# Token stages with two norms: ScalarE's second root placed ahead of the copies of the older chunk's projections

## The chip, the cores and the metric

The kernel runs on one core of a Trainium2 chip. The metric is the device time of one execution in microseconds, as the median of several executions of the same program. An engine is named as the profile names it: PE is TensorE (PEld its weight loads), ACT is ScalarE, DVE is VectorE, POOL is GpSimd, SP is SyncE.

## The reference, cut to what matters

Two decoder layers work on x of shape (2, 1024, 256), 2048 tokens in all. Each layer adds to the residual, in turn, a self-attention, a cross-attention on a context of 77 tokens, and a feed-forward part. The last part of the second layer normalises twice: the layer norm in front of it, and an RMS norm inside it.

```python
def _layernorm(x, axis=-1, eps=1e-05):
    m = jnp.mean(x, axis=axis, keepdims=True)
    v = jnp.var(x, axis=axis, keepdims=True)
    return (x - m) / jnp.sqrt(v + eps)

def _rmsnorm(x, w):
    xf = x.astype(jnp.float32)
    rms = jax.lax.rsqrt(jnp.mean(xf * xf, axis=-1, keepdims=True) + EPS)
    return (xf * rms).astype(x.dtype) * w

x = x + _L1_xattn_ref(_layernorm(x), ctx_1024, ctx_1024, mask, ...)
x = x + _L1_ffn_ref(_layernorm(x), ...)
# inside _L1_ffn_ref, with h the layer-normed x that it was given:
# q, k, v = rmsnorm(h, ln1_w) @ wq.T, wk.T, wv.T, 16 heads of 16
```

What the change touches is this place: the residual after the cross-attention's output projection is layer-normed, kept as `Y`, RMS-normed, and projected to queries, keys and values.

## The kernel before, in words

The program is a chain of stages with a barrier after each. Token stages (`token_stage`, tags t0 to t6) carry out everything that is done token by token between two attentions: the output projection of the attention behind, the residual sum, the norm or norms, the projections for the attention ahead. Between them lie attention stages (a0, a1, a3, a4, a5) and expert stages (e2, e6).

A token stage goes through eight chunks of 256 tokens (two tiles of 128). Each engine runs its own program of steps, written by `in_stages` (L83): a step is given three chunks, the newest, the one before it and the one before that. The order of the work on an engine is the order of the lines in that engine's `step`; between engines only semaphores order it. In step n:

- **PE** (block from L626): output projection of chunk n into `psY` (L649); then the feature units of chunk n-2 (L672) and its value rows (L677) into banks `psP`; then the transposes of chunk n-1 (L691). In DVE's and ACT's counting, where the newest chunk is the one that is being normalised, PE makes `psY` one chunk ahead of it.
- **DVE**: residual sum (L836), moments of the newest chunk (L810, L813), in stages with parts the remainder `rr` of the oldest chunk (`rest`, L905), reciprocal of the root (L824), the first normalisation (L855), and with two norms the moments of its result (L810 and L813 again, and for an RMS norm mean squared plus variance, L816 and L818), the second reciprocal (L824), the second normalisation (L880); then the copies of the middle chunk's values out of `psP` (L942). Each step ends in a drain.
- **ACT**: `root(front, 0)` (L703), `second_part` of the oldest chunk (L756), `keep` (L709: the kept copy `Y`), `projections` of the middle chunk, `root(front, 1)` (L703 again), `turned_rows` (L768 and L770, in other stages L765).
- **POOL**: `store_sets` of the oldest chunk: it waits for ACT's `second_part`, subtracts for the third part (L484) and issues the stores (L488); then the store of the middle chunk's values (L502).
- **SP**: loads of the attention's rows, and late in the stage the first loads of the next one.

`projections(middle)` reads each feature unit's bank twice per unit: once to `fo` (L740, f32) and once to `parts` (L742, bf16), and the second gives the bank back (`act_free`). Before the copies it waits for `rest_ready` and for the older stores from the same buffer.

Queries, keys and values of a chunk make six jobs on PE (four feature units, two halves of the values), on RP = 4 banks. So a job waits until the job four before it has been emptied:

```python
if not (c == 0 and n < RP):
    pe.wait_ge(*freed(back, n - RP))
```

`freed` counts ACT's semaphore for feature units and DVE's for values. `root` waits for the moments and writes `sd`, which DVE's `inverse_root` waits for:

```python
act.wait_ge(var_ready, c * passes + q + 1)
act.activation(sd[:], src, ACT.Sqrt, bias=G["eps"][:]).then_inc(sd_ready, 1)
```

`passes` is 2 for two stages. t2 (`norm="ln_ln"`) has a gate and no feature units: `units` is empty and NS is 0. t5 (`norm="ln_rms"`) has four feature units (queries and keys, two each), values of 256 columns, and a kept `Y`. t5 runs from about 1918 to 2005 us of the profiled span.

Of the kernel before, what the change touches and what calls it, by code (L numbers as in the profile page):

```python
# [379 lines left out]
def token_stage(nc, G, tag, weights, *, norm, attn=None, resid=None, units=(), wide=None, heads_group=4, hd=16, outs=None,  # L380
# [14 lines left out]
    passes = 1 if norm in ("ln", "rms") else 2  # L395
    dve_frees = [u >= n_units + n_rot for u in range(NU)]

    with Stage(nc, tag) as st:
# [122 lines left out]
        with st.block() as block:  # L521
# [175 lines left out]
            def _(act):  # L697
                def root(front, q):

                    c, p, r = front  # L700
                    act.wait_ge(var_ready, c * passes + q + 1)
                    src = mv[:, :, 1:2] if not (norm == "rms" or (norm == "ln_rms" and q)) else ms[:, :, 1:2]
                    act.activation(sd[:], src, ACT.Sqrt, bias=G["eps"][:]).then_inc(sd_ready, 1)  # L703

                def keep(front):

                    c, p, r = front
                    act.wait_ge(xn_ready if norm == "ln_ln" else kept_ready, c + 1)
                    act.activation(G["Y"][:, bass.ds(c * CT, CT), :], xn[p][:], ACT.Copy).then_inc(y_kept, 1)  # L709
# [35 lines left out]
                def first_part(back):  # L745

                    c, p, r = back
                    act.wait_ge(rotated, c + 1)
                    wait(act, f_out[p], r * store_per_use)
                    act.activation(parts[p][:, :, 0, :], fo[p][:], ACT.Copy).then_inc(first_cast, 1)  # L750

                def second_part(back):

                    c, p, r = back
                    act.wait_ge(rest_ready, c + 1)
                    act.activation(parts[p][:, :, 1, :], rr[p][:], ACT.Copy).then_inc(second_cast, 1)  # L756

                def turned_rows(front):

                    c, p, r = front  # L760
                    act.wait_ge(turned, c + 1)

                    wait(act, pu_ready, (c - 1) * NU)
                    if fsc is None:
                        act.activation(xT[p][:].rearrange("p k (t q) -> p t k q", q=P), psX[p][:], ACT.Copy  # L765
                                       ).then_inc(xT_ready, 1)
                    else:
                        act.activation(xT[p][:, 0, :].rearrange("p (t q) -> p t q", q=P), psX[p][:, :, 0, :],  # L768
                                       ACT.Copy, scale=fsc[:, 0:1])
                        act.activation(xT[p][:, 1, :].rearrange("p (t q) -> p t q", q=P), psX[p][:, :, 1, :],  # L770
                                       ACT.Copy, scale=fsc[:, 1:2]).then_inc(xT_ready, 1)

                def step(front, middle, back):
                    in_parts = NS and wide is None
                    if front:
                        root(front, 0)
                    if back and in_parts and not rope:
                        second_part(back)
                    if front and keep_y:
                        keep(front)  # L780
                    if middle:
                        projections(middle)
                    if front and passes == 2:
                        root(front, 1)
                    if back and rope:
                        first_part(back)
                    if front:
                        turned_rows(front)
                    if back and rope:
                        second_part(back)  # L790

                in_stages(step)
                if NS and wide is None:
                    store_last(act, 1)
# [2054 lines left out]
```

## Time and profile before

| what | value |
|---|---|
| median of 3 runs | 2729.84 us |
| lowest and highest of them | 2726.03 and 2733.44 us |
| the profiled execution's own time | 2742.19 us |
| its span in the profile | 2740.5 us |
| PE busy | 2372.9 us, 87% |
| DVE busy | 1609.1 us, 59% |
| ACT busy | 1132.7 us, 41% |
| POOL busy | 1024.0 us, 37% |

The span runs from the first to the last instruction; the execution's own time has a little around it (1.7 us). Busy shares are means over stages that have different limits, so for a change inside one stage its timeline is what counts. In a timeline a row gives the start, the length of the stretch, engine, line, operation, what is written and read, how many instructions were merged into the row, and in brackets the idle time before it with what ended it.

### The profile page before, as it was taken

How to read it: one execution, taken by the hardware profiler on the slowest of the kernel's cores; microseconds unless marked ns; L12 is line 12 of the kernel's file. 1: busy time of each engine (PE TensorE's matmuls, PEld its weight loads, DVE VectorE, ACT ScalarE, POOL GpSimd, SP SyncE). 2: the span in 40 equal slices, each digit the busy share in tenths (PEclk: the TensorE clock that was granted, in tenths of full speed). 3: DMA queues.
4: the chain of work that ended last, by engine and by line, in shares of the span. 5: the costliest groups of instructions: out<-in, count | busy, mean ns of one | idle time of the engine just before them, and what ended most of it. 6: DMA issues, size and time to landing. Idle time of an engine off the chain costs nothing. (4 is left out here: it accounts for less than half of the span.)

```text
span 2740.5 us, 44861 instructions
## 1 busy us (share of the span) xinstructions
PE 2372.9 (87%) x16088; PEld 1261.4 (46%) x16088; DVE 1609.1 (59%) x2652; ACT 1132.7 (41%) x2058; POOL 1024.0 (37%) x799
## 2 busy tenths in 40 slices
PE   6688997777897986999999999867869999968998
PEld 5533335245786762333333333732622222247887
DVE  6778864664443324666666664356779999663222
ACT  3446664331002331444444444233536777812221
POOL 3621004212441113776777777131440000015665
PEclk9889998567999997999999999965979999969999
DMA  4432203438995562122222221433431211046665
GB/s 148 133 83 63 73 20 95 95 93 242 332 334 157 192 204 91 59 91 79 70 86 82 84 73 52 152 109 71 123 107 38 58 39 37 13 117 184 187 194 147
DMA packets 233134, 315.50 MB, mean 115 GB/s; under 512 B 56838, under 2 KB 173856, under 8 KB 232447
## 3 DMA queue, kind: packets, MB, share of 16 engines
q1 hardware_dynamic: 192412, 243.02, 28.1%
q0 software_dynamic: 35232, 66.39, 10.1%
q10 hardware_dynamic: 5314, 3.78, 0.6%
q8 instruction: 107, 1.75, 0.3%
q14 instruction: 69, 0.56, 0.1%
HBM read 215.59 MB, written 96.83 MB: 114 GB/s over the span
## 5 line engine op out<-in xcount | busy, mean ns | idle before, releaser
L1731 ACT ACTIVATE a_probs<-a_cols 128x512 f32<-128x512 f32 (+3 forms) x896 | 445.2, 549 | 242.4 <-PE a_cols L1669 161.8
L1745 DVE TENSOR_REDUCE a_mxw<-a_rows 128x2 f32<-128x1024 f32 (+1 forms) x448 | 475.1, 1098 | 63.4 <-PE a_rows L1627 38.4
L2179 DVE TENSOR_REDUCE a_mxw<-a_rows 128x2 f32<-128x1024 f32 x256 | 313.3, 1224 | 207.9 <-PE a_rows L2007 206.1
L2158 ACT ACTIVATE a_probs<-a_cols 128x1024 f32<-128x1024 f32 x256 | 261.5, 1024 | 267.0 <-PE a_cols L2036 249.5
L1988 POOL TENSOR_TENSOR a_sums<-a_sums,a_probs 128x1024 f32<-128x1024 f32 x128 | 309.7, 2420 | 103.5 <-ACT a_probs L2158 90.9
L2483 PE MATMUL e_psU<-e_xT,e_w 128*128 128x128 f32 (+1 forms) x1472 | 253.0, 331 | 11.6 <-issue 8.3
L2483 PEld LDWEIGHTS e_psU<-e_xT,e_w 128*128 128x128 f32 x1472 | 229.0, 195 | 33.6 <-issue 13.8
L1988 POOL TENSOR_TENSOR a_sums<-a_probs 128x1024 f32<-128x1024 f32 x64 | 150.2, 2347 | 92.7 <-ACT a_probs L2158 92.7
L1669 PE MATMUL a_cols<-a_qs,a_ks 50*128 50x512 bf16 (+7 forms) x1120 | 172.1, 360 | 4.4 <-ACT a_probs L1731 4.4
L1591 POOL DMA_DIRECT2D attn_scratch<-a_on x40 | 19.1, 485 | 418.1 <-DVE a_on L1783 418.0
L2497 PE MATMUL e_psD<-e_w,e_h 128*128 128x256 f32 x736 | 174.0, 379 | 1.1 <-DVE e_h L2654 1.1
L1697 PE MATMUL a_out<-a_probs,a_vs 128*17 128x256 f32 (+4 forms) x2080 | 159.8, 381 | 0.2 <-ACT a_probs L1731 0.2
L2497 PEld LDWEIGHTS e_psD<-e_w,e_h 128*128 128x128 f32 x736 | 134.5, 190 | 17.0 <-DVE e_h L2654 1.5
L2032 PE MATMUL a_cols<-g_first_rows 64*128 64x512 f32 x512 | 134.7, 605 | 0.0
L2007 PE MATMUL a_rows<-g_first_q 64*128 64x512 bf16 x512 | 101.7, 394 | 36.5 <-DVE a_mxw L2179 27.6
L2032 PE MATMUL a_cols<-a_qf,a_kf 64*128 64x512 f32 x512 | 133.1, 598 | 0.0
L672 PE MATMUL t_psP<-t_xT,t3w_wf 128*128 128x256 f32 x512 | 117.1, 390 | 10.6 <-ACT t_xT L765 5.6
L2050 PE MATMUL a_out<-a_probs,g_last_on 128*64 128x512 f32 x512 | 124.9, 609 | 0.0
L2050 PE MATMUL a_out<-a_probs,a_vs 128*64 128x512 f32 x512 | 123.8, 605 | 0.0
L1627 PE MATMUL a_rows<-a_ks,a_qs 48*128 48x512 bf16 (+3 forms) x560 | 104.0, 369 | 21.9 <-DVE a_mxw L1745 21.1
L1310 ACT ACTIVATE a_probs<-a_cols 77x512 f32<-77x512 f32 x128 | 68.8, 587 | 113.4 <-PE a_cols L1272 113.4
L1669 PE MATMUL a_cols<-g_first_q,g_first_k 48*128 48x512 bf16 (+7 forms) x672 | 105.7, 376 | 10.3 <-DMA g_first_q<-a_nparts 8.4
(319 smaller groups left out, 3777.9 us busy)
## 6 DMA issues: line engine op xcount, KB each, us to landing
e_w<-in_w SPq DMA_DIRECT2D x46, 1024.0 KB
e_w<-in_w SPq DMA_DIRECT2D x69, 512.0 KB
qk_wide_scratch<-t_f SPq DMA_DIRECT2D x32, 512.0 KB
a_qs<-q_scratch SPq DMA_DIRECT2D x216, 64.0 KB, 2.2
vw_scratch<-t_v SPq DMA_DIRECT2D x8, 1040.0 KB
g_first_rows<-attn_scratch SPq DMA_DIRECT2D x32, 256.0 KB, 3.2
qk_wide_bf_scratch<-t_fb POOLq DMA_DIRECT2D x32, 256.0 KB
g_first_q<-qk_wide_bf_scratch SPq DMA_DIRECT2D x32, 256.0 KB, 3.0
```

Of the source, the lines that this page charges most:

```text
L672: mm = pe.matmul(psP[slot][:, 0:C], wfs[:, k, m * P:(m + 1) * P], xT[p][:, k, :], start=(k == 0), stop=(k == KD - 1))
L1669: return pe.matmul(dst[e][:, 0:512 - c0], ks[p][rows, kind, hp, i // 4, i % 4 * P:(i % 4 + 1) * P], qs[p][rows, kind, hp, w, c0:512], star ...
L1697: mm = pe.matmul(psO[32 * h:32 * h + VC, a:b], vs[p][:, i, h, :], pr[ug % RING][:, h, a:b], start=i == 0, stop=ug + 1 == unit_end[w] and p ...
L1731: act.activation(pr[ug % RING][:, 2 * hp + e, c0:512], psC[(2 * at + e) % 3][:, 0:512 - c0], ACT.Exp, scale=scale).then_inc(ex_done, 1)
L1745: dve.tensor_reduce(mxw[w][:, a, hp, :, t % 4:t % 4 + 1], src[:, :, 0:n], AX.X, ALU.max).then_inc(s_free, 1)
L1988: pool.tensor_tensor(acc[:], acc[:] if n else pr[i - 1][:], pr[i][:], ALU.add).then_inc(added, 1)
L2032: pe.matmul(dst[:, h, :], kf[p][rows, i * P:(i + 1) * P], qf[p][rows, queries], start=True, stop=False)
L2050: mm = pe.matmul(psO[w][64 * h:64 * (h + 1), :], vs[p][:, i, (hd + 1) * h:(hd + 1) * h + hd], pr[i][:, h, :], start=(i == 0), stop=(i == Q ...
L2158: act.activation(pr[i][:], psC[i % 2][:], ACT.Exp, scale=scale).then_inc(ex_done, 1)
L2179: dve.tensor_reduce(mxw[:, j % 2, :, j // 2:j // 2 + 1], psR[:], AX.X, ALU.max).then_inc(s_free, 1)
L2483: mm = pe.matmul(psU[n % 4][:, 0:R], ws[i][:, k, m * P:(m + 1) * P], xT[p][:, k, :], start=(k == 0), stop=(k == KD - 1))
L2497: mm = pe.matmul(psD[t][:], h[p][:, m, t * P:(t + 1) * P], w2s[i][:, m, :], start=(m == 0), stop=(m == NF - 1))
```

## The change

In ACT's `step`, `root(front, 1)` is issued before `projections(middle)` instead of after it. Nothing else is changed: the same instructions, tiles, semaphores and counts.

```diff
                         second_part(back)
                     if front and keep_y:
                         keep(front)
+                    if front and passes == 2:
+                        root(front, 1)
                     if middle:
                         projections(middle)
-                    if front and passes == 2:
-                        root(front, 1)
                     if back and rope:
                         first_part(back)
                     if front:
```

## Rows read from the trace of the kernel before

**Rows 1.** The page's head.

```profile
span 2740.5 us, 44861 instructions
```

**Rows 2.** Timeline of DVE in t5, the step of chunk 4.

```profile
1955.60 0.69 DVE L836 TENSOR_TENSOR g_X<-t_psY,g_X 128x512 f32<-128x512 f32 x1
...
1960.70 1.19 DVE L816 TENSOR_TENSOR t_ms<-t_mv 128x2 f32<-128x2 f32 x1
1961.96 0.16 DVE L818 TENSOR_TENSOR t_ms<-t_ms,t_mv 128x2 f32<-128x2 f32 x1
1962.58 0.17 DVE L824 RECIPROCAL t_rs<-t_sd 128x2 f32<-128x2 f32 x1 [0.46 <-ACT t_sd L703]
...
1963.36 0.74 DVE L942 COPY g_last_values<-t_psP 128x256 f32<-128x256 f32 x2
1964.19 0.69 DVE L836 TENSOR_TENSOR g_X<-t_psY,g_X 128x512 f32<-128x512 f32 x1
```

**Rows 3.** Timeline of POOL in the same step.

```profile
1959.74 2.12 POOL L484 TENSOR_TENSOR t_parts<-t_r,t_parts 128x1024 bf16<-128x1024 f32 x1 [2.40 <-ACT t_parts L756]
```

**Rows 4.** Timeline of ACT in the same step.

```profile
1960.09 0.37 ACT L740 ACTIVATE t_f<-t_psP 128x256 f32<-128x256 f32 x1
1960.35 0.38 ACT L742 ACTIVATE g_last_parts<-t_psP 128x256 bf16<-128x256 f32 x1
...
1962.19 0.35 ACT L703 ACTIVATE t_sd<-t_ms,g_eps 128x2 f32<-128x2 f32 x1
```

**Rows 5.** Timeline of PE in t5: chunks 0 and 2, then the step of chunk 4.

```profile
1935.38 1.89 PE L677 MATMUL t_psP<-t5w_wv,t_xT 128*128 128x256 f32 x8
...
1952.19 1.99 PE L677 MATMUL t_psP<-t5w_wv,t_xT 128*128 128x256 f32 x8 [0.39 <-ACT t_parts L742]
...
1960.78 1.99 PE L677 MATMUL t_psP<-t5w_wv,t_xT 128*128 128x256 f32 x8
1963.49 0.66 PE L691 MATMUL t_psX<-g_ident,t_xn 128*128 128x128 f32 x4 [0.72 <-DVE t_xn L880]
1963.99 1.89 PE L649 MATMUL t_psY<-t5w_wo,g_first_rows 128*128 128x256 f32 x8
```

**Rows 6.** Windows: length, busy of PE, PEld, DVE, ACT, POOL, then granted clock.

```profile
1940.00:1995.00 55.00, 47.36 (x217) 37.71 (x217) 44.00 (x116) 32.60 (x90) 37.42 (x37) 1.00 0.57 168
```

**Rows 7.** Timeline of DVE in t5: fronts 0 to 2, and the stage's end.

```profile
1926.59 0.16 DVE L818 TENSOR_TENSOR t_ms<-t_ms,t_mv 128x2 f32<-128x2 f32 x1
...
1936.46 0.17 DVE L824 RECIPROCAL t_rs<-t_sd 128x2 f32<-128x2 f32 x1 [3.56 <-ACT t_sd L703]
...
1937.23 0.74 DVE L942 COPY t_v<-t_psP 128x256 f32<-128x256 f32 x2
1938.07 0.69 DVE L836 TENSOR_TENSOR g_X<-t_psY,g_X 128x512 f32<-128x512 f32 x1
...
1996.68 0.42 DVE L942 COPY g_last_values<-t_psP 128x256 f32<-128x256 f32 x1 [0.37 <-PE t_psP L677]
```

**Rows 8.** Timeline of ACT in t5, the second root of front 0.

```profile
1926.78 0.30 ACT L703 ACTIVATE t_sd<-t_ms,g_eps 128x2 f32<-128x2 f32 x1 [1.01 <-DVE t_ms L818]
```

**Rows 9.** Timeline of PE in a3, where it had sat idle, and in t6.

```profile
1136.73 0.39 PE L2007 MATMUL a_rows<-g_first_q 64*128 64x512 bf16 x2 [1.82 <-DVE a_mxw L2179]
1137.05 1.94 PE L2050 MATMUL a_out<-a_probs,a_vs 128*64 128x512 f32 x8
...
1258.60 0.39 PE L2007 MATMUL a_rows<-g_first_q 64*128 64x512 bf16 x2 [2.09 <-DVE a_mxw L2179]
1258.91 2.82 PE L2050 MATMUL a_out<-a_probs,g_last_on 128*64 128x512 f32 x8
...
2415.11 3.78 PE L649 MATMUL t_psY<-t6w_wo,g_first_rows 128*128 128x256 f32 x8
```

**Rows 10.** Windows, columns as in rows 6.

```profile
1134.00:1140.00 6.00, 4.18 (x22) 1.17 (x20) 4.47 (x5) 2.52 (x3) 3.62 (x2) 1.00 0.17 44
1259.80:1263.10 3.30, 3.30 (x12) 1.03 (x10) 1.23 (x2) 0.60 (x1) 0.19 (x1) 0.50 0.24 79
```

## The prediction

> **What bounds the kernel now.** I read the page's head for the span, then the timelines of the engines in the one stage where the edit moves work. Of the two stages with `passes == 2`, t2 has no feature units: NS is 0, `projections` issues nothing there but one wait on weights that PE has already waited for, and the swap is empty. All of the change lies in t5, eight chunks of about 9 us in a span of 2740.5 us [rows 1].
>
> In t5 the step is periodic. VectorE begins chunk 4 at 1955.60 and chunk 5 at 1964.19: a period of 8.59 us [rows 2]. The reader is to see in rows 2 that VectorE is nearly a closed chain: its only wait is 0.46 us for the second root, and its small multiply L816 takes 1.19 us. In the same pattern L818, equal in shape, takes 0.16 us. L816 begins at 1960.70 inside GpSimd's L484, which runs 1959.74 to 1961.86, and ends at 1961.89, with it [rows 2, 3]. So the second variance is ready only at 1961.96 + 0.16 = 1962.12. ScalarE's second root starts at 1962.19, right after the last copy of the older chunk [rows 4]. The copies fill a time in which the root could not have run anyway. PE sat idle 0.72 us a step, waiting for the normalised rows, at a granted clock of 1.00 through the stage's middle [rows 5, 6].
>
> **What moves.** No instruction is added or removed; `sd`'s two users keep their order. The second Sqrt moves ahead of the eight copies (L740, L742 of four units) in each of fronts 1 to 7; front 0 has no older chunk. No DMA is issued by ScalarE in these steps and no other queue's order changes. What is new is that the copies are queued behind the wait for the second variance.
>
> **The gain.** Alone, a Sqrt starts 0.03 us after its input (1926.59 + 0.16 to 1926.78) and lasts 0.30 us [rows 7, 8]. So in steady steps the root starts at 1962.15 instead of 1962.19, and behind no copies ends some 0.05 us sooner: about 0.1 us a step at most. Only in front 1, where GpSimd has no work yet, is the root really late: VectorE waited for it 3.56 us [rows 7]. But there PE's values of chunk 0 hold both the transposes and VectorE's copies: they end at 1935.38 + 1.89 = 1937.27 [rows 5]. VectorE's last copy could start at 1937.30, and with 0.42 us for it and 0.09 for the drain (both as in the steady step) the next front begins at 1937.81 instead of 1938.07 [rows 7]. The gain of front 1 is 0.26 us.
>
> **The cost.** `freed` makes PE's fifth job of a chunk, the first half of its values, wait until ScalarE has emptied the bank of unit 0. In the kernel before it starts at 1960.78, right behind L742's end at 1960.35 + 0.38 = 1960.73, and once PE waited 0.39 us for just that copy [rows 4, 5]. This wait is what grows. With the root first: root at 1962.15, next activation 0.20 us on (an estimate: its 0.30 less 0.1, since L740 and L742 overlap by 0.11), L740's 0.26 us to L742's start, L742 0.38 us: bank free at 1962.99, values at 1963.04. That is 2.26 us later than 1960.78 [rows 4, 5]. The values take 1.99 us, to 1965.03; VectorE sees them 0.03 us on, copies the second half in 0.42 us and drains 0.09: chunk 5 begins at 1965.57 instead of 1964.19 [rows 2, 5, 7]. PE's transposes stand behind the values in PE's queue and slide by the same: blocks on PE overlap by 0.16 (1963.49 + 0.66 against 1963.99), so they start at 1964.87 instead of 1963.49. **Each steady step becomes 1.38 us longer, 9.97 instead of 8.59.** The cover that the copies had, the time of VectorE's L816 stall, is gone. Of the 2.26 us only 0.88 are absorbed: PE's idle 0.72 and the overlap of 0.16.
>
> The other bound, GpSimd's L484, keeps its place in the step, since it follows L756, which stays ahead of the root. So the stall stays. That VectorE's next front would wait for PE's y is excluded: it began at 1964.19, while the y block of 1963.99 had 1.89 us to go and is for the front after [rows 2, 5].
>
> Fronts 2 to 7 are six such steps. The last one counts in full, because after it PE's last products and VectorE's last value copies (at 1996.68, waited for 0.37 us) carry the delay to the stage's end [rows 7]. A barrier ends the stage and nothing overlaps it. The sum at full clock: 6 x 1.38 - 0.26 = **+8.0 us**.
>
> **The clock.** PE's work in a step is 8.59 - 0.72 = 7.87 us, so in 9.97 us it would be idle 2.10 us, all of it in one gap ahead of the values. The trace has close relatives, amid dense products at full clock. After a gap of 1.82 us at 1136.73 eight 512-column matmuls took 1.94 us, with 1.00 granted. After one of 2.09 us at 1258.60 the same eight took 2.82 us, and 0.50 was granted from 1259.8 to 1263.1 [rows 9, 10]. 0.50 is the level of 1.2 GHz, 1.00 that of 2.4 GHz. The gap of 2.10 us is nearest to the one of 2.09, price 2.82 - 1.94 = 0.88 us. The bounds are 0 (as after 1.82 us) and, were all eight value matmuls at half clock, 3.78 - 1.89 = 1.89 us, the difference of two equal blocks of L649 at either level [rows 5, 9]. A slow stretch also makes PE's own work longer and so the next gap shorter, so I take four of the six gaps: 4 x 0.88 = +3.5 us. The Trainium skill, TensorE: Matmul & The Clock Gate, section "HAM oscillation — how this bites in real kernels", asks only that idle gaps longer than this one be avoided. By that rule no clock is lost here and the sum would stay at 8.0; the row at 1258.60 speaks against it.
>
> **Forecast.** 8.0 + 3.5 = +11.5 us. The profiled execution took 2742.19 us, 12.35 us above the median of the three runs shown, 2729.84 us. The sum turns 2742.19 into 2753.7, and the median into **2741.3 us** (+0.42%). What can be told from no change is 0.3%, 8.2 us.
>
> **Rivals.**
> - Clock stays full (0.25). For it: the gap after 1.82 us was harmless, and this one is at its margin. Against it: the row of 2.09 us. +8.0 us, 2737.8 us, just at the edge of what can be told.
> - Half clock over all the values in each of six steps (0.12). 8.0 + 6 x 1.89 = +19.3 us, 2749.2 us. For it: the gap returns each period; against it: longer work closes the next gap.
> - Not slower (0.08): L816's stall goes. Its place is the meeting of L816 with L484. If any shift lets L816 start before L484, it takes 0.16 instead of 1.19, the root starts 1.03 us sooner, and the step is 8.94 instead of 9.97: 0.35 x 6 - 0.26 = +1.8 us, 2731.7 us, no difference. It decides once L484 starts over 0.96 us later in the step (1960.70 - 1959.74) [rows 2, 3]. Against it: the chain L905, L756, L484 is untouched. By the Trainium skill, SBUF — State Buffer, section "SBUF: two separate sides", GpSimd's instruction holds the shared ports whole and a two-input VectorE instruction waits for its end; by that the stall stays as long as the order does.
> - The change does nothing (0.05): some unseen limit, such as the copies already waiting for the root's place. Time 2729.8. Against it: PE starts the values within 0.05 us of the copy's end [rows 4, 5].
>
> A gain beyond 0.3% has no mechanism: even all of PE's idle 0.72 us in six steps is 4.3 us.
>
> **How the numbers follow.** The forecast has 0.50. Range: from the clock-stays-full case with some 4 us of spread (the three runs spread 7.4) to the half-clock case: 2734 to 2750; it leaves out the two cases at no difference and little else. Slower by over 0.3%: 0.49 of the forecast, the 0.12 and 0.09 of the 0.25, which sits at the edge: 0.70. Within: the rest but for 0.04: 0.26. Faster: 0.04 for what I don't see.
>
> **What would show it.** Right: in t5 ScalarE's order is L709, L703, then the copies; VectorE's wait before L824 shrinks to 0.36 us and a wait for PE before L942 appears; PE's L677 block is released by L742 after about 2.1 us; the period is 10 us or more; L816 still takes 1.19 us; L677 blocks of 2.5 us and more where the clock fell. Wrong: a period of 8.6 to 9, L677 not waiting, or L816 at 0.16 us. A clock of 1.00 throughout with a period of 9.97 would leave the mechanism and drop the clock's term.

## The result, and the profile after

Four runs of the changed kernel had a median of 2744.72 us (2742.08 to 2748.11) against 2727.94 us (2725.17 to 2733.44) for the kernel before: ratio 1.0047, 95% interval 1.0032 to 1.0062, that is 8.7 to 16.9 us slower. The two medians lie 16.8 us apart, at the upper end of that interval. The forecast was slower by 11.5 us, to 2741.3 us. Two later sets of the same kernel, with twelve and eight runs, gave 1.0032 (1.0015 to 1.0048) and 1.0041 (1.0023 to 1.0058), that is 8.7 and 11.2 us.

The page's head after, which answers to [rows 1]:

```profile
span 2742.3 us, 44857 instructions
```

The spans differ by only 1.8 us, and this must not be read as the cost. The two profiled executions differ in places where the kernels do not. t5's first residual sum came at 1915.11 instead of 1921.90 us, 6.79 us sooner. From t5's last L911 to the end it took 2742.3 - 2007.75 = 734.55 us against 739.65, 5.10 us less. t5 itself took 13.69 us more, and 13.69 - 6.79 - 5.10 = 1.80. So single executions can't be compared whole (35 runs of the kernel before spread from 2723 to 2743 us), but t5 can. The table gives VectorE's steps in t5, from one L836 to the next, and the last from L836 to the end of L911, out of VectorE's timelines. Front n is the step in which chunk n is normalised; the last column is called the tail below, and the sum the stage:

| front | 0 | 1 | 2 | 3 | 4 | 5 | 6 | 7 to L911 | sum |
|---|---|---|---|---|---|---|---|---|---|
| before, us | 6.16 | 10.01 | 8.59 | 8.94 | 8.59 | 8.60 | 8.58 | 19.48 | 78.95 |
| after, us | 6.15 | 9.77 | 11.66 | 10.34 | 9.99 | 9.99 | 9.98 | 24.76 | 92.64 |

The stage's last row on VectorE, in the kernel before and then in the changed one:

```profile
1999.62 1.23 DVE L911 TENSOR_TENSOR g_last_parts<-t_r,g_last_parts 128x1024 bf16<-128x1024 f32 x1 [1.12 <-ACT g_last_parts L756]
```

```profile
2006.52 1.23 DVE L911 TENSOR_TENSOR g_last_parts<-t_r,g_last_parts 128x1024 bf16<-128x1024 f32 x1 [1.12 <-ACT g_last_parts L756]
```

VectorE's timeline after, in front 4's step, answers to [rows 2]:

```profile
1953.03 0.69 DVE L836 TENSOR_TENSOR g_X<-t_psY,g_X 128x512 f32<-128x512 f32 x1
...
1958.13 1.18 DVE L816 TENSOR_TENSOR t_ms<-t_mv 128x2 f32<-128x2 f32 x1
1959.38 0.16 DVE L818 TENSOR_TENSOR t_ms<-t_ms,t_mv 128x2 f32<-128x2 f32 x1
1959.90 0.17 DVE L824 RECIPROCAL t_rs<-t_sd 128x2 f32<-128x2 f32 x1 [0.36 <-ACT t_sd L703]
...
1961.70 0.42 DVE L942 COPY g_last_values<-t_psP 128x256 f32<-128x256 f32 x1 [0.94 <-PE t_psP L677]
1962.50 0.42 DVE L942 COPY g_last_values<-t_psP 128x256 f32<-128x256 f32 x1 [0.37 <-PE t_psP L677]
1963.02 0.69 DVE L836 TENSOR_TENSOR g_X<-t_psY,g_X 128x512 f32<-128x512 f32 x1
```

The reader is to see that the wait for the root shrank from 0.46 to 0.36 us, as intended, while two new waits for PE's values appeared ahead of L942, 0.94 and 0.37 us. L816 still takes 1.18 us. GpSimd's L484, as in [rows 3], still ends with it, at 1957.17 + 2.12 = 1959.29:

```profile
1957.17 2.12 POOL L484 TENSOR_TENSOR t_parts<-t_r,t_parts 128x1024 bf16<-128x1024 f32 x1 [3.17 <-ACT t_parts L756]
```

ScalarE in the same step [rows 4]. The root now waits 1.97 us for the second variance, with the eight copies queued behind it:

```profile
1959.58 0.29 ACT L703 ACTIVATE t_sd<-t_ms,g_eps 128x2 f32<-128x2 f32 x1 [1.97 <-DVE t_ms L818]
1959.78 0.36 ACT L740 ACTIVATE t_f<-t_psP 128x256 f32<-128x256 f32 x1
1960.04 0.37 ACT L742 ACTIVATE g_last_parts<-t_psP 128x256 bf16<-128x256 f32 x1
```

PE [rows 5]: in the steady step, then at the two places where the clock had fallen, fronts 2 and 7:

```profile
1954.47 3.62 PE L672 MATMUL t_psP<-t_xT,t5w_wf 128*128 128x256 f32 x16
1960.47 2.00 PE L677 MATMUL t_psP<-t5w_wv,t_xT 128*128 128x256 f32 x8 [2.37 <-ACT g_last_parts L742]
1962.30 0.60 PE L691 MATMUL t_psX<-g_ident,t_xn 128*128 128x128 f32 x4
...
1938.46 3.68 PE L677 MATMUL t_psP<-t5w_wv,t_xT 128*128 128x256 f32 x8 [2.37 <-ACT g_last_parts L742]
...
1990.78 3.78 PE L677 MATMUL t_psP<-t5w_wv,t_xT 128*128 128x256 f32 x8 [3.25 <-ACT t_parts L742]
1994.35 1.06 PE L691 MATMUL t_psX<-g_ident,t_xn 128*128 128x128 f32 x4
1996.34 5.48 PE L672 MATMUL t_psP<-t_xT,t5w_wf 128*128 128x256 f32 x16 [0.93 <-ACT t_xT L770]
```

The windows of those stretches, columns as in [rows 6], the granted clock third from the end. It is 0.50 (1.2 GHz) over the slow blocks and 1.00 (2.4 GHz) between them, where [rows 6] had 1.00 throughout:

```profile
1938.50:1941.80 3.30, 3.30 (x8) 2.68 (x9) 0.68 (x2) 1.55 (x6) 2.10 (x3) 0.50 0.69 206
1942.00:1989.00 47.00, 34.75 (x165) 28.91 (x163) 36.05 (x95) 23.48 (x61) 25.78 (x26) 1.00 0.49 145
1990.00:1999.50 9.50, 7.80 (x20) 5.95 (x21) 2.86 (x6) 4.92 (x14) 5.58 (x6) 0.50 0.37 112
```

### The profile page after: what moved, and what is told of

Same layout as the page of the kernel before. It is cut to its first block and busy times, and to the rows that moved or that the text cites. A ratio compares the mean times of both kernels' runs of the same rounds, so it can differ in the third digit from the quotient of the medians.

```text
span 2742.3 us, 44857 instructions
## 1 busy us (share of the span) xinstructions
PE 2369.6 (86%) x16084; PEld 1268.5 (46%) x16088; DVE 1606.4 (59%) x2652; ACT 1133.7 (41%) x2058; POOL 1024.1 (37%) x799
## 5 line engine op out<-in xcount | busy, mean ns | idle before, releaser
L672 PE MATMUL t_psP<-t_xT,t3w_wf 128*128 128x256 f32 x512 | 117.1, 391 | 10.4 <-ACT t_xT L765 5.6
```

The source lines that it names most:

```text
L672: mm = pe.matmul(psP[slot][:, 0:C], wfs[:, k, m * P:(m + 1) * P], xT[p][:, k, :], start=(k == 0), stop=(k == KD - 1))
```

## The experiments

Two theories were at hand. **Banks**: the cost is PE's fifth and sixth job waiting for the banks of units 0 and 1, which ScalarE empties only after the root's wait. **Clock**: a second cost comes from PE's gap. Against them stood a rival, that it is the place of the root itself or ScalarE's lateness as a whole that costs, and the prediction's rival, that the meeting of L816 with L484 decides. Step times are read as in the table above.

### Root behind the copies of unit 1 (e1)

```diff
                             ins.then_inc(act_free, 1)
+                            if i == 1 and front and passes == 2:
+                                root(front, 1)
...
                     if middle:
-                        projections(middle)
-                    if front and passes == 2:
+                        projections(middle, front)
+                    if front and passes == 2 and not (middle and NS):
                         root(front, 1)
```

The edit is against the kernel before; `projections` is given `front` as a second parameter. The last line still serves front 0, and t2.

> The second root stands between the copies of unit 1 and of unit 2. Bank theory (the whole cost is PE's values waiting for the banks of units 0 and 1): both banks are free before the root waits, so the values start where they did before the change. The t5 step is 8.5 to 8.6 us, PE's wait before L677 is at most 0.4 us, the clock stays at 1.00 in t5, and the time is that of the kernel before within 1 us (ratio 0.9996 to 1.0003). Rival, position theory (any copy behind the root's wait costs, because ScalarE as a whole is late: the last four copies would push the transposed rows L768 and L770): the step is 9 us or more, +3 us or more.

Measured: steps 8.49, 8.85, 8.49, 8.50, 8.50 us in fronts 2 to 6, stage 78.40 us, ratio 0.9997 (0.998 to 1.0013). ScalarE's timeline shows four copies ahead of the root; PE's shows values that start without a wait:

```profile
1952.42 0.36 ACT L740 ACTIVATE t_f<-t_psP 128x256 f32<-128x256 f32 x1
...
1953.21 0.39 ACT L742 ACTIVATE g_last_parts<-t_psP 128x256 bf16<-128x256 f32 x1
1954.49 0.29 ACT L703 ACTIVATE t_sd<-t_ms,g_eps 128x2 f32<-128x2 f32 x1 [0.89 <-DVE t_ms L820]
1954.70 0.36 ACT L740 ACTIVATE t_f<-t_psP 128x256 f32<-128x256 f32 x1
```

```profile
1953.11 2.00 PE L677 MATMUL t_psP<-t5w_wv,t_xT 128*128 128x256 f32 x8
1955.73 0.66 PE L691 MATMUL t_psX<-g_ident,t_xn 128*128 128x128 f32 x4 [0.63 <-DVE t_xn L882]
```

The whole cost is gone though four copies still stand behind the root's wait. The rival that any copy behind the root's wait costs falls. The steps are 0.1 us shorter than before, which is the root's small gain with none of its cost.

### Root behind the copies of unit 0 (e2)

The same edit with `i == 0`, against the kernel before.

> The second root stands between the copies of unit 0 and of unit 1. Bank theory: the first half of the values starts in time, the second waits for unit 1's bank: free at 1962.98 in the coordinates of chunk 4, second half 1963.03 to 1964.1, VectorE's last copy and drain to 1964.64 instead of 1964.19: step 9.04 us, +0.45 a step, +2.7 us in all, PE idle about 1.2 us a step, clock 1.00. Position theory: between e1 and the change, nearer to the change: +7 us or more. Clock-only theory (the step is longer only where the clock fell): no change, since the gap is short.

Measured: steps 9.14, 9.47, 9.13, 9.13, 9.13 us, 0.54 more than before, where 0.45 was expected. The stage took 82.98 us, 0.9 us of the excess from front 1 (10.89), where the clock rose later (L649 took 3.62 us and L672 4.33 us); ratio 1.0006 (0.9991 to 1.0022), too little to tell in the time. PE's timeline shows the values split in two: the first half starts in time, the second waits for unit 1's copy.

```profile
1962.01 1.13 PE L677 MATMUL t_psP<-t5w_wv,t_xT 128*128 128x256 f32 x4
1964.28 1.13 PE L677 MATMUL t_psP<-t5w_wv,t_xT 128*128 128x256 f32 x4 [1.14 <-ACT g_last_parts L742]
```

So each unit whose copies come after the wait holds back the job that needs its bank, and no other. With none, one, or two units ahead of the root the step is 9.99, 9.13 and 8.50 us.

### PE's gap filled with products of zeros (e3, e9), beside the change (e4, e10)

The edit of e3 and e9 is against the changed kernel; e4 and e10 are the changed kernel as it is.

```diff
+                            if norm == "ln_rms" and n == RP and front and c >= 1:
+                                zero_products(pe, G, psX[front[1]][:].rearrange("p t k q -> p (t k q)"), 9)
                             if not (c == 0 and n < RP):
                                 pe.wait_ge(*freed(back, n - RP))
```

> The changed kernel with nine products of zeros (512 columns, bf16, into the transposes' idle bank) put on PE between a chunk's feature units and its values, so that PE isn't idle while it waits; they do no work of the result. Two-part theory (1.40 us a step from the bank, and 5.6 us from two drops of the clock): the step stays 9.99 us, but the clock stays at 1.00 through t5 and no L677 block takes 3.7 us; from VectorE's first residual sum to L911 the stage takes 77.7 + 8.2 = 85.9 us instead of 91.4; against the change repeated on the same chip some 4 to 6 us less. Bank-only theory (what looked like the clock is part of the wait): 91.4 us as in the change, no gain. If the products run past the wait's end the step is over 10.0 us.

> The changed kernel itself, once more, as the yardstick for the other three on this chip and to see whether the clock falls in the same steps. Two-part theory: step 9.99 us wherever the clock is full; at least one L677 block of 2.5 us or more; +9 to +15 us against before. If the clock's drops depend on when the gap falls, they come in other steps than 2 and 7. Bank-only theory: exactly the same 91.4 us.

Measured in e3: steps 10.00, 10.34, 9.99, 9.99, 10.00 us, tail 20.78, stage 87.02 us to the end of L911; less L911's own 1.23 us that is 85.8 us, for 85.9 expected. PE waits only 0.43 us now, yet the values start no sooner in the step. The clock was 1.00 from 1923 us on, within front 1:

```profile
1952.89 2.11 PE L169 MATMUL t_psX<-g_zerosb 128*128 128x512 bf16 x9
1955.42 2.00 PE L679 MATMUL t_psP<-t5w_wv,t_xT 128*128 128x256 f32 x8 [0.43 <-ACT g_last_parts L744]
```

```profile
1923.00:1996.00 73.00, 65.84 (x309) 50.42 (x308) 50.18 (x129) 38.03 (x104) 41.04 (x42) 1.00 0.45 136
```

Measured in e4, the change itself: stage 89.80 us, with two slow blocks again, but in fronts 2 and 5 (steps 11.26 and 11.51 us). The equal gaps around them did nothing:

```profile
1957.16 1.99 PE L677 MATMUL t_psP<-t5w_wv,t_xT 128*128 128x256 f32 x8 [2.38 <-ACT g_last_parts L742]
...
1967.14 3.51 PE L677 MATMUL t_psP<-t5w_wv,t_xT 128*128 128x256 f32 x8 [2.38 <-ACT t_parts L742]
```

In the time the two were equal in this set: 2739.68 and 2739.55 us, ratios 1.0030 and 1.0032. So both were run once more.

> The changed kernel with nine products of zeros in PE's gap, again, beside the change: is the clock's term seen in the time, not only in a profile? So far the stage took 87.0 us with the gap filled and 89.8 and 92.6 us in two profiles of the change, but the medians of the two were equal. If the drops cost 3 to 5 us in most executions: the median here is at least 2 us under the change's in this set. If they cost that in few executions, or filling costs elsewhere what it gives: within 1 us. In the profile: step 9.99 us, clock 1.00, stage 87.0 us.

> The changed kernel, a third profile and ten more times. Two-part theory: steps of 9.99 us with at least one of 11 us or more, where an L677 block takes 3 us or more; stage 88 to 93 us. Ratio to before 1.003 to 1.005.

Now the filled gap gave 2739.6 us, ratio 1.0028 (1.0015 to 1.0041), the change 2744.51 us, ratio 1.0041 (1.0023 to 1.0058). The profiles repeated: 87.03 us with the gap filled, 92.70 us for the change, with its slow blocks in fronts 2 and 7 as in the first profile. The three profiles of the change cost 5.6, 2.8 and 5.7 us over the filled gap's 87.0. In the times the difference is 0 in one set and in the other 5 us by the medians, 3.6 us by the ratios, and the intervals overlap: shown in the profiles, likely but not settled in the times.

### L816's wait taken away, in three orders (e5, e6, e7)

Mean squared plus variance is made by one tensor-scalar instruction per tile, whose only tile input is `mv`; the arithmetic is the same. It holds for t6 too. The diff is against the kernel before in e5 and e6, which also has e1's edit, and against the changed kernel in e7.

```diff
-                        dve.tensor_tensor(ms[:, :, 0:1], mv[:, :, 0:1], mv[:, :, 0:1], ALU.mult)
-                        dve.drain()
-                        ins = dve.tensor_tensor(ms[:, :, 1:2], ms[:, :, 0:1], mv[:, :, 1:2], ALU.add)
+                        for t in range(CT):
+                            ins = dve.tensor_scalar(ms[:, t, 1:2], mv[:, t, 0:1], mv[:, t, 0:1], mv[:, t, 1:2], ALU.mult, ALU.add)
```

> The kernel before, with mean squared plus variance (L816, L818: two multiplies and adds with two tile inputs each) computed by one tensor-scalar instruction per tile with the same result, so that VectorE needn't wait for GpSimd's L484. Root order as before. Lock theory (L816's 1.19 us is the wait for L484's end): the new instructions take about 0.16 us each, the variance is ready 1.2 us sooner, but now the second root is the one that waits, behind the copies, which end where they did: VectorE waits about 1.5 us before L824 and the t5 step stays 8.5 to 8.6 us. Time as before within 1 us. Rival (the new instruction waits for GpSimd as well): it takes about 1 us and VectorE's wait before L824 stays 0.46 us.

Old order: steps 8.60, 8.94, 8.60, 8.60, 8.59 us, ratio 1.0006 (0.9995 to 1.0017). On VectorE the two new instructions take 0.45 us together, begun at 1954.43 in the middle of L484 (1953.46 for 2.13 us). They do not wait. What was stall before is now a wait for the root behind the copies, 1.42 us:

```profile
1954.43 0.45 DVE L817 TENSOR_SCALAR t_ms<-t_mv 128x1 f32<-128x1 f32 x2
1956.31 0.17 DVE L823 RECIPROCAL t_rs<-t_sd 128x2 f32<-128x2 f32 x1 [1.42 <-ACT t_sd L703]
```

This profile also has a slow block that the kernel before didn't show. Near the end of t5 PE's L672 took 5.41 us, at a granted clock of 0.67 over 1976.00 to 1981.20, though no gap of PE from front 2 up to it was longer than 0.93 us. It cost nothing in the step: the tail was 19.47 us, against 19.48 before.

```profile
1976.00 5.41 PE L672 MATMUL t_psP<-t_xT,t5w_wf 128*128 128x256 f32 x16 [0.93 <-ACT t_xT L770]
```

> The same tensor-scalar form, with the second root between the copies of unit 1 and unit 2. Bank theory and lock theory together: neither VectorE (7.5 us a step) nor the banks hold the step, PE's own work does: step 7.9 us, PE without idle time in t5, stage 6 x 0.7 = 4 us shorter than before, ratio about 0.998. If the new instruction waits for GpSimd too: step 8.5 us as in the run with the root behind unit 1.

Root between units 1 and 2: steps 7.73, 8.62, 7.72, 7.73, 7.90 us; 2729.77 us, ratio 0.9986 (0.9972 to 0.9999). In fronts 2, 4 and 5 PE's blocks follow without idle time; front 5:

```profile
1967.12 3.62 PE L672 MATMUL t_psP<-t_xT,t5w_wf 128*128 128x256 f32 x16
1970.85 1.99 PE L677 MATMUL t_psP<-t5w_wv,t_xT 128*128 128x256 f32 x8
1972.68 0.60 PE L691 MATMUL t_psX<-g_ident,t_xn 128*128 128x128 f32 x4
```

Fronts 2 to 6 took 39.70 us, 3.6 less than before, but 1.4 came back in the tail (20.89 against 19.48 us), and 0.7 in front 1 (10.72 us), where the clock rose later (L672 took 4.16 us). The whole stage took 77.53 us, only 1.42 less. In the tail the last chunk's copies wait for older stores out of the same buffer, 3.17 us where it was 1.19:

```profile
1995.28 0.38 ACT L740 ACTIVATE t_f<-t_psP 128x256 f32<-128x256 f32 x1 [3.17 <-DMA k_scratch<-g_last_parts]
```

> The changed kernel with the tensor-scalar form. Bank theory: the root's wait ends 1.0 to 1.2 us sooner, the banks with it, so the step is 8.8 to 9.0 us: shorter than the change's 9.99, still longer than before's 8.59 (the rival of the prediction, that the root's early place costs nothing once the stall is gone, gave 8.94). PE's gap before the values falls to about 1.3 us and the clock stays at 1.00 in t5. If the new instruction waits for GpSimd too: 9.9 us.

New order: steps 9.03, 9.37, 9.03, 9.03, 9.03 us; ratio 1.001 (0.9993 to 1.0027). PE's gap is 1.41 or 1.42 us, in front 3 1.76, and the clock held through all of these. It fell only in front 7, after the longest gap:

```profile
1972.27 2.00 PE L677 MATMUL t_psP<-t5w_wv,t_xT 128*128 128x256 f32 x8 [1.41 <-ACT t_parts L742]
...
1990.68 3.62 PE L677 MATMUL t_psP<-t5w_wv,t_xT 128*128 128x256 f32 x8 [2.30 <-ACT t_parts L742]
```

Even where the root has nothing of GpSimd's left to wait for, its place ahead of the copies costs 0.4 us a step against before and 1.3 us against the place behind unit 1.

### The better version again (e11)

> The tensor-scalar form with the second root between units 1 and 2, again, since the first interval reached 0.9999. If the steps of 7.7 us are worth what they show (5 steps x 0.87 us, and VectorE's shorter path in t6), the ratio is 0.997 to 0.999 once more; if the first result was chance, it is 1.000.

2729.18 us, ratio 0.999 (0.9977 to 1.0002), steps 7.72, 8.60, 7.72, 7.72, 8.21, stage 77.08 us, 1.87 less than before. The two sets point the same way, 1 to 1.4 thousandths under the kernel before; the second alone doesn't exclude no difference. These ratios stand for 3.8 and 2.7 us, and t5's stage accounts for 1.4 and 1.9 of them in the profiles; where the rest comes from is not shown. Set beside the change's ratios of 1.0032 to 1.0047, both are faster beyond their intervals.

### Root first in fronts 0 and 1 only (e8)

```diff
-                    if front and passes == 2:
+                    if front and passes == 2 and not back:
                         root(front, 1)
                     if middle:
                         projections(middle)
+                    if front and passes == 2 and back:
+                        root(front, 1)
```

> The root first only in fronts 0 and 1, behind the copies from front 2 on: the part of the change that should help, alone. Bank theory: front 1's step 9.77 instead of 10.01 us, all others 8.59; the stage 0.25 us shorter than before, not to be told in the time. Position theory: no difference to that, so this run measures only the size of the gain.

A single execution: fronts 2 to 6 at 8.59, 8.95, 8.59, 8.60, 8.60 us as expected. Front 1 took 10.62 us, not 9.77. Its L649 block took 3.62 us and L672 4.06 us, so the clock rose later in this execution, and the gain of 0.25 us can't be read from it. The change's own profiles had 9.77, 9.77 and 9.76 us. The old order took 10.01 us in e5 as well, where the clock rose as early as in the change (L672 3.62 us in both), so the gain is the root's.

## Why the prediction was right

- **Front 1's gain.** Said: 0.26 us. Measured: 10.01 to 9.77, 0.24 us.
- **The root's gain in steady steps.** Said: about 0.1 us at most, from 0.46 us of wait to 0.36. The wait is 0.36 us, and e1 shows the 0.1 us where nothing takes it back.
- **The bank.** Said: each of six steps 1.38 us longer, 9.97 us. Measured: 9.99 us in fronts 4 to 6, 1.40 in front 3. e1 and e2 show that the root's place costs through the banks of the units behind it and, with both banks free, nothing; e3 that the step is the same when PE isn't idle.
- **The sum at full clock.** Said +8.0 us. e3's stage is 87.02 - 78.95 = 8.07 us longer, and its times 1.0030 and 1.0028 (e3 and e9), 8.2 and 7.6 us; the medians give 6.3 and 8.1.
- **The gap and the clock.** Said: a gap of 2.10 us. It was 2.37. PE's transposes no longer wait: they overlap the values' block by 0.17 us (1960.47 + 2.00 against 1962.30) and took 0.60 instead of 0.66 us, so PE's own work fills less of the step than the 7.87 us that I took from a step with its idle time subtracted. Said: four slow blocks at 0.88 us, 3.5 us. Measured: two in each of three profiles. Their L677 blocks were 1.3 to 1.8 us longer, and the stage 5.6, 2.8 and 5.7 us longer than with the gap filled. The dearest was front 7's: after a gap of 3.25 us the clock stayed at 0.50 over L677, L691 and into the next L672 (5.48 us), and the tail took 24.76 us where it was 20.78 with the gap filled, 4.0 us for one drop. This term was mis-sized: too many drops, each priced too low, and the long stretch at the stage's end not foreseen. There the gap is the largest, because no y block stands ahead of the feature units. That 3.5 us lies between 2.8 and 5.7 is luck, since the two errors pull against each other; the 8.0 us beside it is not.
- **The rivals.** Clock stays full: what e3 forces, not what the change does by itself. The change does nothing: no, PE's values waited 2.37 us for L742. Half clock in each step: no, 12 of the 18 gaps of fronts 2 to 7 in three profiles did nothing, and these were 2.32 to 3.26 us long. L816's stall goes: no, 1.18 us in each step; and e7 puts the price at 9.03 us a step, where the rival said 8.94. The Trainium skill's clock rule (TensorE: Matmul & The Clock Gate, "HAM oscillation — how this bites in real kernels"), which would let gaps like these pass, does not hold here: slow blocks followed gaps of 2.30, 2.37 and 2.38 us. Its rule of the shared ports (SBUF — State Buffer, "SBUF: two separate sides") agrees: the two-input L816 ends with L484, and the one-input form in e5 runs through it in 0.45 us.

## What to carry to other kernels

Before a short instruction is moved ahead on an in-order engine, ask what then stands behind its wait, and which of those hand back a buffer that another engine is waiting for; here two of four units did, and the right place was behind these two. A stall can hide another: with the two-input multiply replaced the old order gained nothing, because the root was then late; the root's new place alone gave 0.1 us, and both edits together shortened the step from 8.59 to 7.7 us. Where a change opens a gap on TensorE such as these, 2.3 us and more in each step, price the clock as well as the gap, and expect the drops to come and go between executions.

## What the runs showed that I had not expected

Whether a gap costs the clock was not decided by its length. After 2.38 us one L677 block took 3.51 us and its neighbour 1.99 us. In the three profiles of the change the slow blocks came in fronts 2 and 7, 2 and 5, and 2 and 7 again, and a gap of 3.26 us in e4 was followed by full clock. What decides it stays open. Nor does it take a long gap: of the seven profiles in which every gap in fronts 2 to 7 stayed under 2 us (before, e1, e2, e5, e6, e8, e11), e5's had a slow block, after 0.93 us. So the runs show that the gaps make drops more frequent, six in three profiles of the change and none in the two with the gap filled, and not that a gap is needed for one. Nine products of zeros in the gap, 2.11 us of work for nothing, were enough to keep the clock at 1.00 in both runs with them.
